# A transformer tower on one core: three rotating score banks, the turn of the maxima outside the maxima's ring, and later places for the normalisations

## What is computed

```
h = patches of x, a 16-point real DFT, a linear map    # 16 items x 1024 tokens x 64
h = h + attention0(layernorm(h))     # 8 heads of 8; a bias of relative position
h = h + ffn0(layernorm(h))           # 2 layers, each shared + routed by group of tokens
h = h + attention1(layernorm(h))     # 8 heads of 8
h = h + moe(layernorm(h))            # 8 experts, gelu, sum of the 2 best by gate
```

## Time and profile before

| what | value |
|---|---|
| time, median of 3 runs | 4210.63 us (4209.2 to 4213.39) |
| the profiled execution's own time | 4208.61 us |
| its span in the trace | 4206.8 us |
| its mean granted clock of PE | 0.983 |
| PE busy | 3919.8 us, 93% |
| DVE busy | 2902.9 us, 69% |
| ACT busy | 2727.7 us, 65% |
| POOL busy | 859.5 us, 20% |

### The profile page before, as it was taken

One profiled execution on the slowest core, in us unless ns is written; L12 is line 12 of the kernel. 1 busy time (PEld: TensorE's weight loads), 2 busy tenths in 40 slices (PEclk: granted clock), 3 DMA queues, 4 the chain that ended last, 5 costly groups with the idle time before them and its releaser, 6 DMA issues.

```text
span 4206.8 us, 62368 instructions
## 1 busy us (share of the span) xinstructions
PE 3919.8 (93%) x21509; PEld 1301.6 (31%) x21509; DVE 2902.9 (69%) x4956; ACT 2727.7 (65%) x4896; POOL 859.5 (20%) x1263
## 2 busy tenths in 40 slices
PE   6988999999999999999999999999999999999896
PEld 3223323232332323323232332323323233332222
DVE  4866857677675766857677775766857677676661
ACT  0656767667676666767667676666767667676564
POOL 4122212121211312212121211312212121211211
PEclk7999999999999999999999999999999999999998
DMA  5113201212121122201212121122201211111100
GB/s 103 37 31 57 40 20 32 53 37 42 32 41 36 31 42 49 42 19 31 53 37 41 32 41 36 31 41 49 42 19 31 52 38 42 32 31 26 30 2 6
DMA packets 119068, 156.37 MB, mean 37 GB/s; under 512 B 24847, under 2 KB 66575, under 8 KB 118717
## 3 DMA queue, kind: packets, MB, share of 16 engines
q1 hardware_dynamic: 118753, 152.38, 17.7%
HBM read 120.01 MB, written 29.36 MB: 36 GB/s over the span
## 4 chain that ended last, share of the span: by engine, by line
PE 67%; ACT 10%; DVE 8%; issue 7%; POOL 3%; DMA 1%; SPq 1%; POOLq 0%; ACTq 0%; DVEq 0%
PE acc L871 17%; PE st L857 17%; PE nat L837 16%; DVE tile_max L1257 5%; PE side L802 3%; PE side L699 2%; ACT hidden L1032 2%; ACT prob L1061 2%; PE side L676 2%; PE side L788 2%; PE side L756 1%; ACT hidden L977 1%; DVE ln_s L1162 1%; POOL centred L1345 1%; PE side L721 1%
## 5 line engine op out<-in xcount | busy, mean ns | idle before, releaser
L1257 DVE TENSOR_REDUCE tile_max<-nat 128x1 f32<-128x512 f32 x4096 | 2598.2, 684 | 1140.3 <-PE nat L837 1120.4
L1061 ACT ACTIVATE prob<-st 128x512 f32<-128x512 f32 x4096 | 2297.6, 596 | 1332.4 <-PE st L857 1279.3
L857 PE MATMUL st<-q_rows,k_rows 99*128 99x512 bf16 x4096 | 1570.9, 384 | 71.6 <-ACT prob L1061 55.4
L837 PE MATMUL nat<-k_rows,q_rows 96*128 96x512 bf16 x4096 | 1447.5, 385 | 56.2 <-DVE tile_max L1257 40.5
L871 PE MATMUL acc<-prob,v_padded 128*32 128x512 f32 x8192 | 1095.5, 607 | 1.0 <-ACT prob L1061 1.0
L857 PEld LDWEIGHTS st<-q_rows,k_rows 99*128 99x128 bf16 x4096 | 397.9, 97 | 1316.8 <-ACT prob L1061 1035.9
L837 PEld LDWEIGHTS nat<-k_rows,q_rows 96*128 96x128 bf16 x4096 | 401.4, 98 | 595.5 <-DVE tile_max L1257 348.3
L1417 POOL TENSOR_SCALAR max_parts<-neg_max 128x16 bf16<-128x16 f32 x128 | 26.3, 206 | 1664.7 <-DVE neg_max L1264 1204.5
L871 PEld LDWEIGHTS acc<-prob,v_padded 128*32 128x32 f32 x8192 | 161.4, 108 | 338.3 <-issue 278.1
L1342 POOL TENSOR_SCALAR ln_s<-ln_s 128x8 f32<-128x8 f32 x64 | 13.0, 203 | 974.0 <-DVE ln_s L1162 974.0
L802 PE MATMUL side<-hidden,w 128*64 128x512 f32 x512 | 136.5, 616 | 0.0
(11 more groups left out here) (129 smaller groups left out, 2106.7 us busy)
## 6 DMA issues: line engine op xcount, KB each, us to landing
q_rows<-q_scratch SPq DMA_DIRECT2D x576, 64.0 KB
k_rows<-k_scratch SPq DMA_DIRECT2D x192, 192.0 KB
x_rows<-in_x SPq DMA_DIRECT2D x62, 512.0 KB, 6.8
q_scratch<-hidden SPq DMA_DIRECT2D x32, 384.0 KB
k_scratch<-hidden SPq DMA_DIRECT2D x96, 128.0 KB
group_weights<-in_routed SPq DMA_DIRECT2D x64, 129.0 KB, 2.2
q_rows<-max_rows SPq DMA_DIRECT2D x512, 3.0 KB
out_h<-out_rows SPq DMA_DIRECT2D x16, 256.0 KB, 2.1
```

The lines of the kernel that those rows point to most:

```text
L837: eng.matmul(NAT[place % len(NAT)][:, :], QA[u][0:K_NAT, h, c:c + P], KA[u][0:K_NAT, h, kh * 512:kh * 512 + 512], start=True, stop=True)\
L857: eng.matmul(ST[n % 2][:, :], KA[u][0:K_ALL, h, t * P:t * P + P], QA[u][0:K_ALL, h, half * 512:half * 512 + 512], start=True, stop=True)\
L1061: eng.activation(prob[:, n % TILES, :], ST[n % 2][:, :], ACT.Exp).then_inc(exp_done, 1)
L1257: eng.tensor_reduce(mx[:, q % 2, j // 8, j % 8 // 2, j % 2:j % 2 + 1], NAT[place % len(NAT)][:, :], AX.X, ALU.max).then_inc(nat_free, 1)
```

## The change

Three things are changed, and a few follow from them. **Banks**: two score banks and the second side bank become a ring of three, `RING` (in the listings all of this tensor, the first side bank too, is named `side_st`). `score_ring` walks the whole program once and gives each score tile and each use of the second side bank a bank and its previous user, for whom `bank_wait` waits. A tile takes the free bank that was used longest ago. A side stage takes the one used longest ago and keeps it out of the ring for four tiles (`SIDE_TILES`); while it does, the tiles alternate between two banks. Where a tile's previous user isn't tile n-2, st goes before nat in all four places. **Turn**: it is a side stage `TN` in the ring of scores at the same tile (n mod 32 = 23); the maxima's ring has only nat in it, and DVE copies the rows after, not before, the reduction of that tile. **Schedule**: LN1 of the last norm moves from tile 16 to 18, and in `middle_of` LN1 moves from 11 to 13 and from 47 to 56 (from tiles 144 and 180 of the round to 146 and 189), with what follows. Besides, `FY` uses the first side bank, and gelu is one instruction of 1024 columns for each expert, over two banks.

```diff
-TURN = 5
-RING_USES = SUPER + 1
+TURN = 23
+SIDE_TILES = 4
...
 
-        for dn, name, *more in ((0, "CT"), (5, "OTR"), (8, "PROJ", 0), (11, "LN1", "a"),
-                                (17, "LN2", "a"), (18, "BO"), (25, "TR", "a"), (28, "H1"), (32, "L0"),
-                                (38, "L1"), (44, "WO"), (47, "LN1", "1"), (53, "LN2", "1"),
-                                (61, "TR", "1"), (64, "QK", 1), (68, "QV", 1)):
+        for dn, name, *more in ((0, "CT"), (5, "OTR"), (8, "PROJ", 0), (13, "LN1", "a"),
+                                (20, "LN2", "a"), (21, "BO"), (28, "TR", "a"), (32, "H1"), (37, "L0"),
+                                (43, "L1"), (49, "WO"), (56, "LN1", "1"), (62, "LN2", "1"),
+                                (70, "TR", "1"), (74, "QK", 1), (79, "QV", 1)):
...
-        put(16, "LN1", r - 1, "m")
-        put(22, "LN2", r - 1, "m")
-        put(30, "TR", r - 1, "m")
-        put(33, "GATE", r - 1)
-        put(40, "RANK", r - 1)
-        put(44, "MT", r - 1)
+        put(18, "LN1", r - 1, "m")
+        put(24, "LN2", r - 1, "m")
+        put(31, "TR", r - 1, "m")
+        put(35, "GATE", r - 1)
+        put(41, "RANK", r - 1)
+        put(45, "MT", r - 1)
         put(48, "FW", r - 1)
         for k in range(E + 1):
             put(51 + 3 * k, f"FY{k}", r - 1)
...
+        put(SUPER * q + TURN, "TN", q + 1)
...
+def score_ring():
+
+
+    tile_bank, tile_prev, side_at, side_prev = {}, {}, [], []
+    last, order, held = [None] * 3, [0, 1, 2], [0] * 3
+
+    def take(bank, use):
+        prev, last[bank] = last[bank], use
+        order.remove(bank)
+        order.append(bank)
+        return bank, prev
+
+    for kind, _, n0, side in program_phases():
+        steps = {0: side} if kind == "serial" else side
+        for n in sorted(steps):
+            for name, b, k, *_ in steps[n]:
+                if name == "FW":
+                    last[:] = [("hidden", E * b + E - 1), ("hidden", E * b + E), ("hidden", E * b + E)]
+                    order[:] = [0, 1, 2]
+                if name in SIDE_BANKS and 1 in SIDE_BANKS[name][k]:
+                    tile = n0 + max(n, 0)
...
+                    held[bank] = tile + SIDE_TILES
+                    side_at.append(bank)
+                    side_prev.append(prev)
+            if kind != "serial" and n >= 0:
+                hidden_next = any(x[0] == "FW" for m in (n + 1, n + 2) for x in steps.get(m, ()))
+                free = [bank for bank in order if not (hidden_next and bank == 0) and held[bank] <= n0 + n]
+                tile_bank[n0 + n], tile_prev[n0 + n] = take(free[0], ("tile", n0 + n))
+    return tile_bank, tile_prev, side_at, side_prev
+
...
+            def bank_wait(prev):
+
+                if prev is not None:
+                    by, value = prev
+                    if by == "tile":
+                        eng.wait_ge(exp_done, value + 1)
+                    elif by == "side":
+                        eng.wait_ge(side_free[1], value + 1)
+                    else:
+                        eng.wait_ge(he_ready, value)
+
...
+                bank_wait(SIDE_PREV[n["bank1"] + use])
+                return RING[SIDE_AT[n["bank1"] + use]]
...
                     for e in range(E):
-                        both = SIDE if e % 2 == 0 else (ST[slot % 2], ST[(slot + 1) % 2])
+                        both = SIDE if e % 2 == 0 else RING[1:3]
                         if e == 1:
                             eng.wait_ge(exp_done, at(tile))
                         elif e > 1:
-                            eng.wait_ge(he_ready, at(2 * E * b + 2 * (e - 1)))
+                            eng.wait_ge(he_ready, at(E * b + e - 1))
                         for par, half in enumerate(HALVES):
                             eng.matmul(both[par][:, :], W1[half, e, :], XT[half, :], start=True, stop=False)
                         for par, half in enumerate(HALVES):
-                            eng.matmul(both[par][:, :], MS[half, e, :], MTb[half, :], start=False, stop=True)\
-                                .then_inc(fw_ready, 1)
...
+                eng.matmul(side_bank(n, 1)[:, 0:P], mpart[:, q % 2, :], ident_b[:, :], start=True, stop=True)\
+                    .then_inc(side_full[1], 1)
...
+                bank_wait(TILE_PREV[n0 + n])
                 t, h = i // HEADS, HEADS * g + i % HEADS
-                eng.matmul(ST[n % 2][:, :], KA[u][0:K_ALL, h, t * P:t * P + P],
+                eng.matmul(RING[TILE_BANK[n0 + n]][:, :], KA[u][0:K_ALL, h, t * P:t * P + P],
                            QA[u][0:K_ALL, h, half * 512:half * 512 + 512], start=True, stop=True)\
                     .then_inc(st_ready, 1)
 
...
+                    two_banks = TILE_PREV[n0 + n] == ("tile", n0 + n - 2)
+                    scores_first = n % HEADS >= 2 or not two_banks
                     if scores_first:
-                        scores(kind, it, n0, n, side, found)
+                        scores(kind, it, n0, n)
                     if kind != "last" or q < SUPERS:
...
                 for e in range(E):
-                    both = SIDE if e % 2 == 0 else (ST[slot % 2], ST[(slot + 1) % 2])
...
+                    both = side_pair if e % 2 == 0 else score_pair
+                    eng.wait_ge(fw_ready, at(E * b + e + 1))
+                    eng.activation(HE[:, e, :], both[:, :], ACT.Gelu, bias=b1[:, e:e + 1]).then_inc(he_ready, 1)
...
+            def rows_out(n0, q, n):
+
+                v = over(n0, SUPER) + q
+                eng.wait_ge(maxrow_in[q % 2], at(DMA_MAX * (v // 2)))
+                bk = full(n, 1)
+                eng.tensor_copy(mrow[:, q % 2, :], bk[0:PARTS * 4 * HEADS, 0:P]).then_inc(side_free[1], 1)
...
+                alone(eng.wait_ge(maxrow_in[q % 2], at(DMA_MAX * (v // 2))))
```

More of the change, by code:

```diff
@@ L199, in side_schedule @@
             middle_of(r + 1, 133)
-    put(150, "HO1", r)
+    put(156, "HO1", r)
+    for q in range(2 * SUPERS):
+        put(SUPER * q + TURN, "TN", q + 1)
     for parts in at.values():
@@ L218, in program_phases @@
             first[n + (1 if part[0] == "RL" else 2) * k].append(part)
+    first[-1] = list(side_parts([("TN", 0)]))
+    for q in range(SUPERS):
+        first[SUPER * q + TURN] += side_parts([("TN", q + 1)])
     ending = side_schedule(B - 1, True, False, False)
@@ L230, in program_phases @@
     f1 = side_schedule(B, True, False, False)
-    end += [x for n in sorted(f1) for x in f1[n] if x[0] not in ("SCR", "VC", "RL", "HO1")]
+    end += [x for n in sorted(f1) for x in f1[n] if x[0] not in ("SCR", "VC", "RL", "HO1", "TN")]
     return [
@@ L281, in counted_phases @@
     return out
+def score_ring():
[15 more added lines that the diff above has]
+                    tile = n0 + max(n, 0)
+                    bank, prev = take(max(order, key=lambda k: held[k] > tile), ("side", len(side_at)))
+                    held[bank] = tile + SIDE_TILES
[6 more added lines that the diff above has]
+    return tile_bank, tile_prev, side_at, side_prev
+TILE_BANK, TILE_PREV, SIDE_AT, SIDE_PREV = score_ring()
 def super_of(kind, it, q):
@@ L390, in tower_kernel @@
         NAT = [bank("nat0"), bank("nat1"), bank("nat2")]
-        ST = [bank("st0"), bank("st1")]
+        four = ctx.enter_context(nc.psum_tensor("side_st", [P, 2048], F32))
+        side_pair, score_pair = four[:, 0:1024], four[:, 1024:2048]
+        RING = [four[:, 512 * k:512 * k + 512] for k in (1, 2, 3)]
         ACC = bank("acc")
-        SIDE = [bank("side0"), bank("side1")]
+        SIDE = [four[:, 0:512], RING[0]]
         s_dft = sem("dft_in")
@@ L558, in _, with max_dma @@
             onehot_rows(1)
-            def max_dma(kind, it, n0, q, last=False):
+            def max_dma(kind, it, q, n):
                 a, b, g, half = super_of(kind, it, q)
-                v0 = over(n0, SUPER)
-                turn = RING_USES * (v0 + q + 1) + (0 if last else TURN)
-                alone(eng.wait_ge(nat_free, at(turn + 1)))
+                alone(eng.wait_ge(side_free[1], n["bank1"] + 1))
                 for hh in range(HEADS):
@@ L628, in body @@
                     return
-                if kind == "first":
-                    max_dma(kind, it, n0, 0)
-                for n in range(n_tiles(kind)):
-                    ahead = n + SUPER + LEAD
-                    if ahead % SUPER == TURN:
-                        q = ahead // SUPER - 1
-                        if kind != "last" or q < SUPERS:
-                            max_dma(kind, it, n0, q, last=(kind == "last" and q == SUPERS - 1))
-                    for k, stage in enumerate(side[n]):
-                        side_stage(stage, found[n, k], n0 + n if kind == "first" or kind == "pair" and 0 < it < B - 2 else 0)
+                for n in sorted(side):
+                    for k, stage in enumerate(side[n]):
+                        if stage[0] == "TN":
+                            max_dma(kind, it, stage[1], found[n, k])
+                        else:
```

(22 more changed lines are left out.)

105 lines of the change are left out of this document (45 added, 60 removed), and 2 rows, old and new, of the table SIDE_BANKS.

## The result

The kernel after takes 4196.02 us (median of 11 runs), the kernel before 4209.2 beside it (11 runs): ratio 0.9969, interval 0.996 to 0.9978. It is faster by 13 us, 0.3%, where I had forecast 50; that is just under the 15 to 90 us which I had called the forecast. One of its eleven runs, of 6251.04 us at a mean granted clock of 0.553 (the others have 0.970 to 0.973), is left out of the ratio.

What follows compares the result with a forecast made beforehand. PE's own issue was taken as the bound, with only its stalls to win: gains of 148 us less costs of 14, 12 and 66 left 56, taken as 50, so 4160 us, range 4090 to 4215.

Steps and rivals of the forecast that it cites:

- the clock behind the stall: PE's lower clock after the idle time at tile 215: 1.2 us more in each of 14 rounds.
- Quiet group, nat and st: Third bank cuts PE's stalls: 43 us short nat, 20 long nat, 36 st; a quiet group takes 2.85 us.
- FW: One gelu of 1024 columns in place of two saves 0.7 us for each of 16 items: 11 us gained.
- Rows of maxima at tile 96: At tile 96 the rows already arrive last, so 0.8 us gained from tile 82 on is lost: 12 us.
- The rival with late rows everywhere: Later DMAs make the rows of the maxima come late in all rounds: 4239 us, chance 0.1.
- Turn at 23 and 151: The split no longer stands behind the first half of a norm, so the turn doesn't wait: 28 us gained.
- More room between stages: TR clears ACT's copy of acc and QK waits less: 0.7 us for 14 rounds, 10 us gained.
- TR late: TR becomes some 0.6 us late in the tail and 0.4 in the middle: 14 us lost.
- The meeting: POOL's split of q and k delays the turn at tile 215: 4.7 us in each of 14 rounds, 66 lost.
- The rival without a meeting: POOL's chain ends before PE arrives at tile 215, so that cost is gone: 4094 us, chance 0.12.
- the one in which the third bank brings nothing: PE's stalls at st and nat only move, so 99 us of gain are lost: 4259 us, chance 0.08.
- half the gains: Gains of 148 us shrink to about 100 and the costs stay: 4210 us, no change, chance 0.12.

Runs made afterwards that it cites:

- e9: e2 with one bank of the ring kept for side stages for good, so that score tiles alternate between two; 4162.9 us.
- e7: e2 with the middle part, from LN1 to v, moved as a block by 2 to 4 tiles; 4091.35 us.
- e12: e7 with the tail's six stages (LN1, LN2, TR, GATE, RANK, MT) where the kernel after has them; 4093.26 us.
- e14: e7 with HO1 moved from tile 150 to 156 and, for layer 0, QK from 122 to 123 and QV from 126 to 127; 4076.8 us.
- e13: e7 with six stages of the middle part's first half (LN2, BO, TR, L0, L1, WO) moved one tile, as in the kernel after; 4126.28 us.
- e11: e7 with q, k and v of layer 1 where the kernel after has them (QK at tile 207, QV at 212); 4176.4 us.
- e2: The kernel after with all tile numbers of the old table, keeping the new banks, turn and gelu; 4116.07 us.

## Why the prediction was right in sign and too large

The direction and the mechanisms that I named held; the price of the new table was too low, in two steps of the prediction: the clock behind the stall, and the moved stages that I had taken as free. Measured on the chip, the code wins 91 us and the table takes 80; my sum had 110 less 12 for the first and 42 for the second.

- **Quiet group, nat and st (99 forecast).** 2.85 us is right to 0.01. The third bank alone gave 47 and the remainder of e9 37, 84 in all, from which the 12 at tile 96 are already gone: the total is right, but with luck, since I had put all of it on the third bank and nothing on the turn outside the ring.
- **FW (11).** 10 measured; 1112 ns for one gelu where 1108 was worked out.
- **Rows of maxima at tile 96 (12 lost).** The wait grew by 10.3 us and 11 times, 12 us with 0.16 for each. Some 8 of them stand at tile 96 of the rounds; 2.6 are the first two waits of the program, which grew from 8.1 to 10.8. The rival with late rows everywhere didn't come.
- **Turn at 23 and 151 (28 won).** Both waits are gone. At 151 it stayed (1.48 us a round in e7). At 23 the 1.46 us were given back in full to TR, nat and MT (e12): 1.6 us, where I had booked 0.6 for TR and nothing for the others.
- **More room between stages (10).** It came with the later `QK` and `QV` of layer 0 (e14, 12 to 15 us).
- **TR late (14 lost).** Its two waits, 0.64 and 0.36 us (0.57 and 0.29 idle, and 0.07 each since an f32 matmul starts that much behind the record's end), are 14 us. What I missed is the st and nat behind L1 one tile later: 35 us with TR's second wait in e13, of which the kernel after shows 22. This is the second step that failed: I had looked at norms and q, k, v, and taken every other stage's move as free, without a reason.
- **The meeting (66 lost).** Place and stall are right: 3.66 us (3.50 idle) where I had 3.5. The first step that failed, and the largest single miss, is its second term, "I take 1.2, since the idle time is a little shorter". From the stalled turn to the next PE takes some 25.8 us on average where it takes 22.85 without the fall, 2.9 more. So the low clock cost 41 us in place of 17, and the meeting is 6.6 for each round and 92 in all; e11, by itself, measured 85. My upper bound of 80 was too low as well: the one meeting of before, cost 1.6, and I took this for the most. In e11 six rounds lost about that much, 1.6, and eight lost 2.8 to 3.1. So one round of before could not give the average, and the reason that I gave, the shorter idle time, is not what sorts the rounds.

The stretches from turn to turn, in a round around 2100 us of each trace, add this up (us):

| turns of tiles | e2 | e7 | after | what differs in after |
|---|---|---|---|---|
| 247 to 23 | 27.14 | 27.13 | 25.67 | no wait at 23 |
| 23 to 55 | 40.21 | 40.22 | 41.81 | TR, nat and MT wait |
| 119 to 151 | 30.77 | 29.29 | 28.55 | no wait at 151, QK at 123 |
| 151 to 183 | 30.86 | 30.95 | 32.58 | TR, L1 |
| 183 to 215 | 27.09 | 26.72 | 30.58 | the stall |
| 215 to 247 | 22.85 | 22.86 | 25.62 | the low clock |

The two others (55 to 87, 87 to 119) are equal within 0.1 on average. After against e2 is 5.9 us a round, 14 x 5.9 = 83, where the medians differ by 80. Summed over the 14 rounds and set beside the terms of my sum: the stall is 49 us, as forecast; the low clock 41 for 17; the stretch of TR and L1 24 for 6; that of TR, nat and MT 23 for 8; and the gains, at 23 and from 119 to 151, are 53 for 38. So the costs were 57 us too low, and 15 us of more gain hid a part of it. The pieces put back one by one come to the same: e11, e12, e13 and e14 are 85 + 2 + 35 - 15 = 107 above e7, and after is 105 above it (4196 - 4091). Two small differences cancel in this. The 0.85 us by which e13 is longer from 183 to 215 (its nat wait) isn't there in after, where PE waits for POOL behind it anyway; and the low clock costs after 2.9 us on average and e11 2.3.

The rival without a meeting is excluded by the trace, the one in which the third bank brings nothing by e9, and half the gains by e2. (The sum of half the gains was off: 148 shrunk to 100 leaves 8 us, 4202, not 4210.) The Trainium skill (TensorE: Matmul & The Clock Gate, "HAM oscillation — how this bites in real kernels") reports no further gain from PSUM double-buffering in its kernel. Here a third bank gave 47 us, so what it saw doesn't carry over to this kernel, whose stalls come in part from side work on ACT and DVE.

## What to carry to other kernels

Test a change of buffers and a change of places apart: here the new code was worth 91 us, the third bank 47 of it, and hid that the new places, which had come with it, cost 80. Price a stall of TensorE with what its clock loses behind it; at 3.5 us of idle time that was 1.6 to 3.1 us more. And when an engine serves a deadline (POOL, busy for 20% of the span only, but with 6.9 us of splits in order ahead of it), place long work behind the deadline's item or far enough ahead, and look at each moved stage one tile to either side, since moves of one tile were worth 12 to 35 us.
